# Attention normalised area by area, projection weights scaled on VectorE, and queries shifted by ScalarE, in a small fused attention and expert block

## The reference, cut to what matters

```
y   = channel layernorm of x
q,k = bn(w_qk y), v = bn(w_v y)            # bn: one scale and one shift per channel
cut the 256 positions into 4 areas of 64; per image, area and head (8 heads of 8 channels):
      o = softmax(q k^T / sqrt(8)) v
x   = x + bn(w_p o)
t   = tokens of x;  n = layernorm(t)
logits = n Wr + br; the two best of 8 experts, their weights a softmax over the two
x   = t + sum over the two of weight * (gelu(n_e W1[e] + b1[e]) W2[e] + b2[e])
                                           # n_e = n * ln_g[e] + ln_b[e], 64 -> 256 -> 64
```

## Time and profile before

| | |
|---|---|
| runs | 45.72, 45.22, 45.30 us; median 45.3 |
| profiled execution | 45.26 us, of which the recorded span is 43.4 |
| PE busy | 37.6 us (87%), weight loads 25.1 |
| ScalarE busy | 25.5 us (59%) |
| VectorE busy | 24.9 us (57%) |
| GpSimd busy | 14.8 us (34%) |
| TensorE's granted clock | 1.00 in every stretch asked for |

### The profile page before, as it was taken

One profiled execution on the slowest core, in us unless ns is written; L12 is line 12 of the kernel. 1 busy time (PEld: TensorE's weight loads), 2 busy tenths in 40 slices (PEclk: granted clock), 3 DMA queues, 4 the chain that ended last, 5 costly groups with the idle time before them and its releaser, 6 DMA issues.

```text
span 43.4 us, 1198 instructions
## 1 busy us (share of the span) xinstructions
PE 37.6 (87%) x430; PEld 25.1 (58%) x430; DVE 24.9 (57%) x98; ACT 25.5 (59%) x63; POOL 14.8 (34%) x30
## 2 busy tenths in 40 slices
PE   0999979949999997699569999999999999999700
PEld 1246667336468894668259937855865676664500
DVE  0001640795999949121998929999946940466410
ACT  3900248252969999394025999399579979900000
POOL 5856256299100000009149770029300000058000
DMA  0366799510000000000000000000000000000022
GB/s 0 61 193 228 169 290 321 241 49 0 0 15 0 0 0 0 0 0 15 0 0 8 0 8 0 0 0 0 0 15 0 0 0 0 0 0 0 0 61 60
DMA packets 1237, 1.88 MB, mean 43 GB/s; under 512 B 272, under 2 KB 848, under 8 KB 1232
## 3 DMA queue, kind: packets, MB, share of 16 engines
q1 hardware_dynamic: 1232, 1.82, 13.7%
HBM read 1.68 MB, written 0.13 MB: 42 GB/s over the span
## 4 chain that ended last, share of the span: by engine, by line
PE 63%; DVE 11%; issue 6%; POOL 6%; DMA 5%; ACT 1%; SPq 1%; DVEq 0%; POOLq 0%; ACTq 0%
PE two L925 19%; PE two L942 18%; PE two L824 5%; DMA par<-params 5%; PE two L793 5%; DVE rzs L533 4%; POOL bnr L254 2%; PE two L804 2%; POOL qaff L290 2%; PE two L719 2%; PE two L906 2%; POOL rstd L259 2%; PE two L773 1%; ACT probT L376 1%; PE two L951 1%
## 5 line engine op out<-in xcount | busy, mean ns | idle before, releaser
L402 ACT ACTIVATE hg<-two,par 128x256 f32<-128x256 f32 x32 | 12.1, 490 | 1.7 <-PE two L925 1.7
L925 PE MATMUL two<-xe,w1s 64*128 64x256 f32 x64 | 8.4, 394 | 0.1
L942 PE MATMUL two<-hg,w2s 128*64 128x256 f32 x64 | 8.0, 387 | 0.0
L719 PE MATMUL two<-warm 128*128 128x512 bf16 x16 | 6.0, 491 | 1.0 <-POOL warm L240 1.0
L925 PEld LDWEIGHTS two<-xe,w1s 64*128 64x128 f32 x64 | 5.8, 186 | 1.8 <-issue 1.2
L264 POOL TENSOR_TENSOR rstd<-var,neghalf 128x2 f32<-128x2 f32 x4 | 2.8, 716 | 8.8 <-DVE var L545 8.8
L942 PEld LDWEIGHTS two<-hg,w2s 128*64 128x64 f32 x64 | 4.1, 136 | 2.9 <-issue 0.5
L626 DVE SCALAR_TENSOR_TENSOR yg<-two,par,gates 128x256 f32<-128x256 f32 x8 | 3.8, 480 | 3.0 <-PE two L942 3.0
L278 POOL TENSOR_SCALAR xe<-xn,par 128x256 f32<-128x256 f32 x6 | 3.5, 589 | 4.7 <-DVE xn L551 4.7
L719 PEld LDWEIGHTS two<-warm 128*128 128x128 bf16 x16 | 1.7, 125 | 2.9 <-issue 1.6
L285 POOL TENSOR_TENSOR acc<-yg 128x256 f32<-128x256 f32 x1 | 0.7, 732 | 7.8 <-DVE yg L626 7.8
(11 more groups left out here) (105 smaller groups left out, 61.0 us busy)
## 6 DMA issues: line engine op xcount, KB each, us to landing
w1s<-w SPq DMA_DIRECT2D x1, 512.0 KB, 5.5
w2s<-w SPq DMA_DIRECT2D x1, 512.0 KB, 6.1
wq<-wqkv SPq DMA_DIRECT2D x1, 256.0 KB, 3.3
xs<-x_split SPq DMA_DIRECT2D x1, 193.0 KB, 2.4
out<-res SPq DMA_DIRECT2D x2, 64.0 KB, 1.6
cst<-consts SPq DMA_DIRECT2D x1, 110.5 KB, 3.2
wp<-wproj SPq DMA_DIRECT2D x1, 32.0 KB, 2.9
par<-params SPq DMA_DIRECT2D x1, 30.0 KB, 2.1
```

What stands on the lines that cost most here:

```text
L402: act.activation(hg[:, n, k, i, :], H[n % 2][i][:, k * B * NH:(k + 1) * B * NH], ACT.Gelu, bias=par[:, c:c + 1]).then_inc(a_g, 1)
L719: pe.matmul(scratch[:, :], warm[:, :], warm[:, 0:1].broadcast_to((P, 512)), start=True, stop=True)
L925: mm = pe.matmul(H[n % 2][i][:, k * B * NH:(k + 1) * B * NH], w1s[rows, c:c + P], xe[rows, f, p, :], start=True, stop=True)
L942: mm = pe.matmul(Y[n % 2][i * C:(i + 1) * C, 0:B * NH], w2s[:, chunk(p, k, i), :], hg[:, n, k, i, :], start=(k == 0), stop=(k == CE - 1))
```

## The change

Nine edits, the core of the diff below.

1. `OT` is now a bank for each area's place in its half, and `sum_inverse` and `normalise` go area by area, on 64 columns each: four of each instead of two.
2. The projection weights come as `w_p` transposed, 128 rows of 64. `scale_rows` (PE) transposes a broadcast column of the batchnorm scale; DVE multiplies (`scaled_wp`), sums the rows and subtracts the mean (`centred_wp`), ahead of `k_scaled(0)`. POOL's `projection_scale`, PE's `scale_wp` and ScalarE's `scaled_wp` go. `shift_of_v` shrinks to one product, and `centre_shift` is another.
3. `q_shifted(0)` moves to ScalarE, `q_shifted(1)` to POOL.
4. DVE: `centred1` ahead of `bn_shift`; `k_scaled(1)` behind `k_masked(1)`.
5. PE: both `var1_rows` ahead of the projections; `project_v` behind `scores(3)`; `turn(3)` ahead of `centre_residual(0)`; fills are placed anew.
6. ScalarE: `v_blocks(0)` behind `exp(1)`, `v_blocks(1)` behind `exp(3)`; `turned(2)`, `turned(3)` ahead of `squares2(0)`; `gelu_table` behind `centred2(0)`.
7. `RB2[0]` moves from bank 4 to banks 2 and 3; `router1(0)` and `normed2(0)` stand right behind `normalise(3)`.
8. `expert_input(0, 2)` and `(0, 3)` move from POOL to DVE, in between the router's steps; `added(1, 0)` moves from POOL to DVE.
9. `spread2(1)` ahead of `gate_rows(0)`; `gate_rows(1)` ahead of `hidden(1, 0)`; `expert_out(0, 2)` behind `hidden(1, 1)`; `normed2(1)` ahead of the four `gates_spread(0, ...)`; `mix` steps and `added` steps shift to suit.

```diff
@@ -132,7 +132,7 @@
-        rzs = sb("rzs", [P, HALVES, NH])
+        rzs = sb("rzs", [P, AREAS, T])
@@ -175,7 +175,7 @@
-        RB2 = [bank[4][:, 0:B * NH].rearrange("p (b n) -> p b n", b=B), two[3][:, :, 0:NH]]
+        RB2 = [two[1][:, :, P:2 * P], two[3][:, :, 0:NH]]
@@ -290,32 +290,22 @@
-            def projection_scale():
-                pool.wait_ge(l_wp, 16)
-                pool.wait_ge(v_bn, 5)
-                pool.tensor_scalar(wpr[:, :], wp[:, 0:P], bnst[0:C, 3:4], None, ALU.mult).then_inc(wpr_ready, 1)
...
             norm1(1)
-            q_shifted(0)
-            projection_scale()
+            q_shifted(1)
             k_masked(2)
...
             expert_input(0, 1)
-            expert_input(0, 2)
-            expert_input(0, 3)
             norm2(1, 0)
...
             expert_input(1, 2)
-            added(1, 0)
             added(1, 1)
@@ -415,25 +400,24 @@
             k_out(0)
+            k_out(1)
             q_out(0)
             q_out(1)
-            k_out(1)
+            q_shifted(0)
             k_shifted()
-            q_shifted(1)
-            v_blocks(0)
-            v_blocks(1)
             exp(0)
             exp(1)
-            scaled_wp()
+            v_blocks(0)
             turned(0)
...
             exp(3)
-            gelu_table()
-            squares2(0)
+            v_blocks(1)
             turned(2)
             turned(3)
+            squares2(0)
             centred2(0)
+            gelu_table()
             centred2(1)
@@ -528,14 +512,17 @@
-            def sum_inverse(f):
-                dve.wait_ge(p_o, AH * (f + 1))
-                dve.reciprocal(rzs[:, f, :], OT[f][:, 2 * P:2 * P + NH]).then_inc(v_rz, 1)
-            def normalise(f):
-                dve.wait_ge(p_o, AH * (f + 1))
-                dve.wait_ge(v_rz, f + 1)
-                dve.scalar_tensor_tensor(out=on[:, f, :], in0=OT[f][:, 0:NH], scalar=bnst[:, 2:3], in1=rzs[:, f, :],
+            def sum_inverse(a):
+                f, i = a // AH, a % AH
+                dve.wait_ge(p_o, a + 1)
+                dve.reciprocal(rzs[:, a, :], OT[i][:, 2 * P + f * T:2 * P + (f + 1) * T]).then_inc(v_rz, 1)
+            def normalise(a):
+                f, i = a // AH, a % AH
+                dve.wait_ge(p_o, a + 1)
+                dve.wait_ge(v_rz, a + 1)
+                dve.scalar_tensor_tensor(out=on[:, f, i * T:(i + 1) * T], in0=OT[i][:, f * T:(f + 1) * T],
+                                         scalar=bnst[:, 2:3], in1=rzs[:, a, :],
                                          op0=ALU.mult, op1=ALU.mult).then_inc(v_on, 1)
@@ -547,12 +534,16 @@
+                if f == 0:
+                    dve.wait_ge(p_lg, 1)
...
+                if f == 0:
+                    dve.wait_ge(p_rb2, 1)
@@ -633,51 +624,79 @@
+            def scaled_wp():
+                dve.wait_ge(l_wp, 16)
+                dve.wait_ge(p_wps, 1)
+                dve.tensor_tensor(wps[:, 1, :].rearrange("p (k o) -> p k o", k=2), wp[:, None, :].broadcast_to((P, 2, C)),
+                                  MISC[:, 0:P].rearrange("p (k o) -> p k o", k=2), ALU.mult).then_inc(v_wps, 1)
+            def centred_wp():
+                dve.wait_ge(v_wps, 1)
+                dve.tensor_reduce(wsum[:, :], wps[:, 1, 0:C], AX.X, ALU.add).then_inc(v_wps, 1)
+                dve.wait_ge(v_wps, 2)
+                dve.scalar_tensor_tensor(out=wps[:, 0, :], in0=wsum[:, 0:1].broadcast_to((P, P)), scalar=-1.0 / C,
+                                         in1=wps[:, 1, :], op0=ALU.mult, op1=ALU.add).then_inc(v_wps, 1)
             def projected_shift():
...
                     .then_inc(v_ptot, 1)
+            def centred_shift():
+                dve.wait_ge(p_pt, 2)
                 dve.tensor_copy(cpt[:, :], MISC[:, 386:387]).then_inc(v_ptot, 1)
...
             bn_mean()
-            bn_shift()
             centred1(1)
             centred1(0)
+            bn_shift()
             bn_softmax_scale()
...
             variance1(1)
+            scaled_wp()
+            centred_wp()
             k_scaled(0)
...
             k_masked(0)
-            k_scaled(1)
-            k_masked(1)
             q_scaled(1)
             normed1(0)
+            k_masked(1)
+            projected_shift()
+            k_scaled(1)
             normed1(1)
...
             score_max(1)
+            centred_shift()
             score_sub(0)
...
             score_sub(3)
-            projected_shift()
             sum_inverse(0)
+            sum_inverse(1)
             normalise(0)
+            normalise(1)
+            sum_inverse(2)
             variance2(0)
-            sum_inverse(1)
-            normalise(1)
+            normalise(2)
+            sum_inverse(3)
+            normalise(3)
+            router1(0)
             normed2(0)
+            router2(0)
             expert_input(0, 0)
-            router1(0)
-            router2(0)
             router3(0)
+            expert_input(0, 3)
             router4(0)
+            expert_input(0, 2)
             router5(0)
@@ -686,28 +705,29 @@
             router4(1)
+            normed2(1)
             gates_spread(0, 0)
...
             router5(1)
-            normed2(1)
-            mix(0, 0)
             expert_input(1, 0)
...
             gates_made(1)
+            mix(0, 0)
             mix(0, 1)
-            mix(0, 2)
-            added(0, 0)
-            added(0, 1)
             gates_spread(1, 0)
...
             gates_spread(1, 3)
+            mix(0, 2)
             mix(0, 3)
+            added(0, 0)
+            added(0, 1)
             added(0, 2)
...
             mix(1, 1)
+            added(1, 0)
             mix(1, 2)
@@ -763,6 +783,8 @@
+                if f == 0:
+                    pe.wait_ge(v_ptot, 2)
@@ -820,28 +842,29 @@
                                 rows = slice(b * C + q * Q, b * C + (q + 1) * Q)
-                                at = kind * 2 * P + i * T
-                                mm = pe.matmul(OT[f][rows, at:at + T],
+                                at = kind * 2 * P + f * T
+                                mm = pe.matmul(OT[i][rows, at:at + T],
                                                ones[:, s, :] if kind else vblk[:, a, b, 2 * q + s, :],
...
-            def scale_wp():
-                pe.wait_ge(wpr_ready, 1)
+            def scale_rows():
+                pe.wait_ge(v_bn, 5)
                 pe.wait_ge(l_cst, 16)
-                pe.wait_ge(l_wq, 16)
-                pe.wait_ge(a_v, 2)
-                pe.matmul(MISC[:, 0:P], wpr[:, :], wq[0:C, CENTER_D, :], start=True, stop=True)
-                pe.matmul(MISC[:, P:2 * P], wpr[:, :], ident[0:C, None, 0:C].broadcast_to((C, 2, C)),
-                          start=True, stop=True).then_inc(p_wps, 1)
+                pe.wait_ge(v_xc, 2)
+                pe.wait_ge(a_sq, 1)
+                pe.transpose(MISC[:, 0:P], bnst[:, 3:4].broadcast_to((P, P)), ident).then_inc(p_wps, 1)
             def shift_of_v():
-                pe.wait_ge(v_bn, 5)
-                pe.wait_ge(a_wps, 1)
-                pe.matmul(MISC[:, 384:385], wps[0:C, 1, :], bnst[0:C, 6:7], start=True, stop=True)
-                pe.matmul(MISC[:, 386:387], wps[0:C, 0, :], bnst[0:C, 6:7], start=True, stop=False)
-                pe.matmul(MISC[:, 386:387], wq[0:C, CENTER_D, :], bnst[0:C, 7:8], start=False, stop=True)\
+                pe.wait_ge(v_wps, 1)
+                pe.matmul(MISC[:, 384:385], wps[0:C, 1, :], bnst[0:C, 6:7], start=True, stop=True)\
+                    .then_inc(p_pt, 1)
+            def centre_shift():
+                pe.wait_ge(v_ptot, 1)
+                pe.matmul(MISC[:, 386:387], xs[:, CENTER:CENTER + P], ptot[:, 0:1], start=True, stop=True)\
                     .then_inc(p_pt, 1)
@@ -880,7 +903,9 @@
-                if f == 1:
+                if f == 0:
+                    pe.wait_ge(v_var2, 2)
+                else:
@@ -899,7 +924,7 @@
-                    pe.wait_ge(v_on, 2)
+                    pe.wait_ge(v_on, AREAS)
@@ -918,6 +943,7 @@
+                    pe.wait_ge(v_xn2, 1)
@@ -931,7 +957,7 @@
-                    pe.wait_ge(v_xn2, 1)
+                    pe.wait_ge(v_on, AREAS - 1)
@@ -977,59 +1003,60 @@
             fill(bank[2])
+            fill(bank[2])
             var1_rows(0)
+            var1_rows(1)
+            scale_rows()
+            project_k(0)
+            project_k(1)
+            project_q(0)
+            project_q(1)
+            spread1(0)
             fill(bank[2])
-            project_k(0)
-            var1_rows(1)
-            project_q(0)
-            project_k(1)
-            project_q(1)
-            fill(bank[2])
-            spread1(0)
             spread1(1)
+            shift_of_v()
+            scores(0)
+            scores(1)
+            fill_idle()
+            centre_shift()
             fill_idle()
             fill_idle()
-            fill_idle()
-            scores(0)
-            scores(1)
+            scores(2)
+            scores(3)
             project_v(0)
             project_v(1)
```

(42 more changed lines are left out.)

## The result

The changed kernel takes 44.16 us in the median of 4 runs (44.11 to 44.30), the kernel before 45.31 (45.22 to 45.72). The ratio is 0.973, with a 95% interval of 0.968 to 0.979. The profiled execution took 44.30 us with a span of 42.5, against 45.26 and 43.4. Some executions of most kernels here took over 1.5% longer than the same kernel's fastest, in part with TensorE longer at its lower clock level; the ratios and the medians of the experiments leave them out, and the profiles of e5, e8 and e9 are of such executions.

What follows compares the result with a forecast made beforehand. Bound by a nearly all-TensorE expert stretch of 16.9 us, so by how early hidden(0, 0) starts. From 45.26, 1.60 gained there, 0.30 lost at gate_rows(1) and 0.18 regained make 1.48: 43.8 us, range 43.2 to 44.8.

Steps and rivals of the forecast that it cites:

- The front: Up to the first row maximum: reordered steps start it at 9.88 instead of 10.45, a gain of 0.57 us.
- Where the weights go: Three new weight instructions fill VectorE's gap ahead of kr, 6.42 to 7.2, and cost nothing if ended by 7.5.
- The shift on ScalarE: Query shift takes 0.40 where POOL took 0.77; scores(0) can start at 8.47, but scores(1) waits for mask(1), 9.23.
- Softmax to xn: From exps through attention to the second layernorm: normed2(0) at 20.20 instead of 21.80, a gain of 1.60 us.
- the stall of turned(2) behind squares2(0): On ScalarE, turned(2) and turned(3) wait from 16.7 to 18.62 before the change; called the largest stall that goes.
- The gain of 0.79 at `variance2(0)`: First half's second-layernorm variance on VectorE starts at 18.42 instead of 19.21.
- The reciprocal's estimate: Softmax-sum reciprocal on 64 columns: 0.16 fixed plus 6.2 ns a column, 0.56 us.
- the rival of dear reciprocals: Reciprocals on 64 columns take 0.956 like 128, so xn comes at 21.2 and the total is 44.8; chance 0.07.
- the area split does nothing: In normalising: centre_projected(0) waits for both areas and v_blocks(1) anyway, so most of the gain is the order.
- The wait at gate_rows(1): In the experts: TensorE, there at 28.14, waits for VectorE's gates until 28.45, a loss of 0.3 us.
- The 0.18 gained back at the pair of 2.11: In the experts: the pair at 33.93 takes 1.93 instead of 2.11, as the gelu is no longer late.
- The slower rival: The weights' transfer lands late and blocks VectorE ahead of k_scaled(0); 45.7 if it takes 6.1; chance 0.05.

Runs made afterwards that it cites:

- e5: Changed kernel with one of the two fills ahead of var1_rows(0) taken out; 44.09 us, ratio 0.970.
- e8: Changed kernel with the projection weights' work moved off the front, centred1 ahead of bn_scale, one fill less, and e4b's order; 44.28 us, ratio 0.974.
- e9: Changed kernel with the query shifts put back, half 0 on POOL and half 1 on ScalarE; 44.20 us, ratio 0.976.
- the control: Changed kernel run once more, unchanged, beside the other runs on the same chip; 44.10 us, ratio 0.971.
- e1: Changed kernel with its area split taken back, one reciprocal and one normalising of 128 columns per half; 44.54 us, ratio 0.981.
- e3: Changed kernel with squares2(0) put back ahead of turned(2) and turned(3) on ScalarE; 45.41 us, ratio 1.002.
- e4: Changed kernel with gate_rows(1) behind hidden(1, 1) instead of ahead of hidden(1, 0); 44.15 us, ratio 0.977.
- e2: Kernel before with only the new ScalarE and TensorE order at the softmax's end; 44.65 us, ratio 0.983.
- e4b: Changed kernel with gate_rows(1) between hidden(1, 0) and hidden(1, 1); 43.88 us, ratio 0.968.
- e10: e8 with projected_shift moved behind score_max(0) and centred_shift behind score_sub(0); 44.28 us, lowest 43.78, ratio 0.970.

## Why the prediction was right, and where it was off

The forecast was 43.8 (43.2 to 44.8); 44.16 was measured. Of a gain of 1.5 there came 1.15. By its own steps (starts in us, profiled execution; "normalised" and "ends" are ends, the reciprocal is a duration):

| step | forecast | measured |
|---|---|---|
| kr | 7.50 | 7.94 |
| first rowmax | 9.88 | 10.44 |
| exp(2) | 14.60 | 15.11 |
| reciprocal on 64 columns | 0.56 | 0.557 |
| first half normalised | 16.41 | 16.94 |
| POOL's powers, second layernorm | 18.66 | 18.92 |
| xn | 20.20 | 20.59 |
| hidden(0, 0) | 21.11 | 21.51 |
| hidden(0, 2) | 25.22 | 25.53 |
| gate_rows(1) | 28.45 | 28.94 |
| last expert_out ends | 38.16 | 38.71 |

**The front: a mis-sized term.** The gain of 0.57 at the first rowmax measured 0.01 in the profiled execution. Counted from the row that waits for the parameters it measured 0.31: the rowmax came 7.14 after that row before (3.31 to 10.45) and 6.83 in the changed kernel (3.61 to 10.44; 6.82 in the control). So 0.26 of the missing 0.56 is my count, and 0.30 goes with the landing, which I had carried over from one profile. Counted the same way, the last `expert_out` ends 1.23 earlier than before, where I had 1.48.

The count: in the changed kernel `kr` starts 4.33 after that row (3.61 to 7.94, 3.45 to 7.78, e1 3.35 to 7.68, e3 3.38 to 7.71, e9 3.33 to 7.66; e4 4.32), with the order of before 4.57 (3.31 to 7.88) and 4.56 (e2, 3.37 to 7.93). So the order of the front gains 0.24 there. I had 4.19: 0.14 too short, mostly `spread1(0)`, 0.1 later than I had it behind the projections. The other 0.12 lies behind `kr`: the rowmax came 2.50 after it, where I had 2.38.

The landing isn't the only thing that varies. e4b has the same front, and its `kr` comes 4.60 after the row (timeline of e4b; that row stands at 3.32):

```profile
4.80 1.06 PE L739 MATMUL two<-warm 128*128 128x512 bf16 x2
...
6.24 0.30 PE L858 MATMUL two<-cst,bnst 128*128 128x128 f32 x1
...
7.92 0.29 DVE L481 TENSOR_TENSOR kr<-ks,two 128x128 f32<-128x128 f32 x1 [0.40 <-PE two L765]
```

`scale_rows` (L858) starts 2.61 or 2.62 after the row in the six others, which is the batchnorm chain; here it starts 2.92 after it, since both fills ran at TensorE's lower level. In the profile of the changed kernel both fills did so too, and `scale_rows` starts at 6.22. So there the late landing and the late rise would each have given this `kr`, and the 0.30 can't be put down to the landing alone.

**Where the weights go** was right: 0.44 of cover was left, and e8 and e10 show that other places are dearer. **The shift on ScalarE** was right in that scores(1) decides; e9 shows 0.1.

**Softmax to xn: right in the main.** The forecast said that the stall of turned(2) behind squares2(0) was the largest that goes, and e2 and e3 show what its order is worth. But turned(3) didn't wait there, as I had read: its transposes stood behind `centre_projected(0)` on TensorE (timeline of before), ended at 18.80, and their eviction ran straight behind turned(2), which ended later.

```profile
18.14 0.66 PE L804 MATMUL two<-cst,prob 128*128 128x128 f32 x4
```

So by that trace ScalarE's order alone would have freed area 2 only; the change altered both queues. The gain of 0.79 at `variance2(0)` measured 0.47 (18.74 against 19.21), and e2 shows that the order gives none of it (19.27). Of 0.56 by which the rowmax was later, 0.26 was left at POOL's powers and 0.39 at xn. The reciprocal's estimate was exact (0.56 against 557 ns), and the rival of dear reciprocals fell. The remark that most of the gain is the order holds (e2), but not that the area split does nothing: e1 gives it 0.4. I had reckoned that `centre_projected(0)` waits for `v_blocks(1)` anyway. With the large reciprocal it waits for the normalising instead: in e1 it starts at 17.28, right behind 17.13, which is 0.33 later than in the control, counted from the landing.

By the Trainium skill ("VectorE: DVE Perf Modes", the hardware budget of the 8-slice walkthrough), its repeat count taken as 8 cycles an element, I had an estimate of 0.66 for 64 columns. The rows say 0.557 for 64 and 0.956 for 128, which is 6.2 ns a column, so the measurement decides against that reading.

**Experts.** The wait at gate_rows(1) was forecast at 0.3, and TensorE idled for 0.37. It came 0.2 later still, and for a reason that I didn't have (timeline of the changed kernel, from 26 us):

```profile
26.12 1.62 POOL L278 TENSOR_SCALAR xe<-xn,par 128x256 f32<-128x256 f32 x3 [1.66 <-DVE xn L540]
...
27.32 0.57 DVE L573 TENSOR_TENSOR eq<-cst,topi 128x32 f32<-128x32 f32 x2
...
27.81 0.40 DVE L610 TENSOR_SCALAR xe<-xn,par 128x256 f32<-128x256 f32 x1
```

Two comparisons of 32 columns took 0.57 instead of 0.28 (they took 0.28 before, at 28.31, when POOL had nothing). The first alone took 0.47 and ended at 27.79, where POOL's third input ended at 27.75. All twelve profiles with this order have the same: 0.46 or 0.47, ended 0.03 or 0.04 behind POOL's third input. In before and e2 the first comparison of the first half meets POOL's third input; it took 0.28 and 0.27, and also ended 0.04 and 0.03 behind it. Where POOL had no input running it took 0.17 or 0.18. The Trainium skill ("SBUF — State Buffer", "SBUF: two separate sides") says that VectorE instructions with two SBUF inputs and GpSimd instructions that read SBUF exclude each other for a whole instruction. These rows fit that. But in the kernel before two other steps with two SBUF inputs ran at 0.17 and 0.18 beside POOL's second input (29.65 to 29.92; that input took 0.63 where others took 0.55), so the cause is argued, not shown; no run here moved POOL's inputs alone. The 0.18 gained back at the pair of 2.11 came as forecast.

The slower rival (the weights' transfer) didn't arise: wp took 2.9 us from issue to landing with its shorter rows too.

## What to carry to other kernels

In strictly ordered queues look first for an instruction whose input has been ready for long behind one that waits: area 2's probabilities stood ready for nearly 2 us behind a table load and a square, area 3's transposes behind a product that waited, and the order alone was worth 0.7 of 1.15 us (e2) or, undone on ScalarE, all of it (e3). Splitting a slow step (0.96) at the points where its inputs arrive is worth another 0.4, while moving work of 0.2 to 0.3 us from a gap of one engine to a busier stretch lost more here than it saved. When you forecast from one profile, count from what varies between executions, here a transfer's landing and the moment at which TensorE's clock rises, and give each its own spread.

## What the runs showed of the hardware

- The row that waits for the parameters' landing differed from execution to execution, for the same transfer: 3.28 to 3.45 us in thirteen profiles, 3.61 in that of the changed kernel.
- TensorE's rise to its upper level differs too, and the granted clock's row doesn't show it. Fills of 512 columns follow each other at 0.43 us at the lower level (1.2 GHz) and at 0.22 at the upper (2.4). In the profile of before the rise lay before the fill at 4.78, in e1 and e4 within the one at 3.51 (0.50 and 0.49 us), in that of after behind the two at 4.79 (1.06 for both). In the profiled execution of e5 it came only beyond 9 us, behind the same busy start (timeline of e5):

```profile
6.45 1.06 PE L774 MATMUL two<-xc,wq 128*128 128x128 f32 x4
7.30 1.06 PE L782 MATMUL two<-xc,wq 128*128 128x128 f32 x4
8.29 0.70 PE L765 MATMUL two<-cst,rstd 128*64 128x128 f32 x4
```

  The projections took 1.06 a pair where the changed kernel has 0.65 and 0.61, `kr` started at 9.11, and the execution took 45.75 us instead of 44.1. The page reads a granted clock of 1.00 for it. In e9's profile the granted clock does fall, to 0.50 from 22 to 24 us, and the `hidden` that starts at 23.25 takes 1.95 there, where the changed kernel has 1.11.
- The gelu table load took 1.28 us and the next activation began at once behind it (18.56 to 19.85). ScalarE's instruction ahead of the load ended at 18.54, so there is no gap on that side either. The drain of about 1.38 us that the Trainium skill ("ScalarE: Activation LUTs", "What ACT_TABLE_LOAD costs") adds to the load at every switch to another set isn't in these traces.
